# Raw-logit routing with GpSimd refining the norm's scale, and the scan's joined products first

## The reference

```python
x = x + 0.5 * ffn(layernorm(x))
x = x + attn(layernorm(x))
x = x + 0.5 * ffn(layernorm(x))
```

## Time and profile before

| | us |
|---|---|
| median of 3 runs (lowest, highest) | 485.46 (484.73, 485.86) |
| the profiled execution's own time | 485.11 |
| its span, first to last instruction | 483.3 |
| PE busy in the span | 430.8 |
| DVE, ACT, POOL busy | 282.0, 244.2, 236.9 |
| mean granted TensorE clock | 0.951 of full |

### The profile page before, as it was taken

The page is one execution under the profiler, slowest core; times in us unless marked ns, Lnnn a source line. Parts: engine busy times, 40 slices in busy tenths (PEclk is TensorE's granted clock), DMA queues, the critical chain, the costliest instruction groups (busy, mean ns, idle before and its releaser), DMA issues.

```text
span 483.3 us, 9854 instructions
## 1 busy us (share of the span) xinstructions
PE 430.8 (89%) x2877; PEld 354.9 (73%) x2877; DVE 282.0 (58%) x1045; ACT 244.2 (51%) x617; POOL 236.9 (49%) x341
## 2 busy tenths in 40 slices
PE   7999699999908989999999999989989599999940
PEld 5544499999903679999999999974644399999930
DVE  3865355555529657677677777754975245555514
ACT  3693255555510445655655556545786145555520
POOL 4167777544410344465555555642047777454530
PEclk9799999999966999999999999999899999999985
DMA  8971325100065200000000000000001417110028
GB/s 228 263 274 52 111 85 173 34 28 28 18 169 169 64 1 1 2 2 2 1 3 0 1 2 2 2 1 1 2 23 50 117 50 205 35 33 28 20 61 218
DMA packets 34514, 30.90 MB, mean 64 GB/s; under 512 B 3838, under 2 KB 30085, under 8 KB 34464
## 3 DMA queue, kind: packets, MB, share of 16 engines
q1 hardware_dynamic: 24608, 19.17, 14.7%
q0 software_dynamic: 4544, 8.47, 5.4%
q10 hardware_dynamic: 5312, 2.62, 2.1%
HBM read 15.55 MB, written 15.61 MB: 64 GB/s over the span
## 4 chain that ended last, share of the span: by engine, by line
PE 79%; DMA 6%; DVE 4%; POOL 4%; issue 3%; ACT 1%; ACTq 0%; SPq 0%; DVEq 0%; POOLq 0%
PE bank L1275 17%; PE bank L710 15%; PE bank L697 14%; PE bank L658 4%; PE bank L568 4%; DMA stage<-y_dram 3%; POOL slots_dram L1402 3%; PE bank L668 2%; PE bank L1069 2%; PE bank L685 2%; PE bank L1144 2%; PE bank L587 2%; DMA stage<-slots_dram 2%; PE bank L1107 1%; PE bank L1129 1%
## 5 line engine op out<-in xcount | busy, mean ns | idle before, releaser
L1656 DVE TENSOR_TENSOR sq<-bank,relu 128x512 f32<-128x512 f32 x86 | 59.4, 691 | 89.2 <-ACT relu L810 88.9
L1407 POOL DMA_INDIRECT y_dram<-y_out,stage x78 | 76.7, 983 | 59.7 <-ACT y_out L836 52.5
L1402 POOL DMA_INDIRECT slots_dram<-rows,slots x64 | 63.4, 991 | 55.5 <-ACT rows L761 27.2
L710 PE MATMUL bank<-proj_w,sq 128*128 x624 | 86.5, 282 | 2.8 <-DVE sq L1656 2.8
L697 PE MATMUL bank<-tileT,tile_w 128*128 128x128 f32 x624 | 83.1, 277 | 0.0
L710 PEld LDWEIGHTS bank<-proj_w,sq 128*128 128x128 f32 x624 | 75.7, 191 | 6.5 <-issue 3.8
L810 ACT ACTIVATE relu<-bank 128x512 f32<-128x512 f32 x94 | 56.0, 595 | 46.4 <-PE bank L697 37.6
L697 PEld LDWEIGHTS bank<-tileT,tile_w 128*128 128x128 f32 x624 | 76.9, 194 | 0.0
L836 ACT ACTIVATE y_out<-bank,stage 128x128 f32<-128x128 f32 x78 | 28.6, 367 | 33.5 <-PE bank L710 33.5
L1270 POOL TENSOR_TENSOR sq<-sq,last_rows 128x128 f32<-128x128 f32 x32 | 14.6, 456 | 53.0 <-DVE sq L1246 53.0
L568 PE MATMUL bank<-ones 128*128 128x512 f32 x34 | 22.2, 801 | 15.5 <-DVE res L1707 12.6
(11 more groups left out here) (268 smaller groups left out, 1020.5 us busy)
## 6 DMA issues: line engine op xcount, KB each, us to landing
slots_dram<-pad SPq DMA_DIRECT2D x2, 2535.0 KB, 13.8
stage<-slots_dram SPq DMA_DIRECT2D x18, 260.0 KB, 5.1
fc_w<-experts SPq DMA_DIRECT2D x1, 2048.0 KB, 20.5
proj_w<-experts SPq DMA_DIRECT2D x1, 2048.0 KB, 24.1
stage<-y_dram SPq DMA_DIRECT2D x8, 256.0 KB, 5.5
stage<-y_dram ACTq DMA_DIRECT2D x8, 256.0 KB, 6.2
y_dram<-y_out,stage POOLq DMA_INDIRECT x78, 2.3
res<-x SPq DMA_DIRECT2D x4, 256.0 KB, 3.9
```

Of the source, the lines that this page charges most:

```text
L710: last = nc.tensor.matmul(bank[4 + i % 2][:, 0:P], sq[:, i % 2, f_cols], proj_w[:, k, f_cols], start=j == 0, stop=j == FJ - 1)
L1402: nc.gpsimd.indirect_dma_start(to, bass.IndirectOffsetOnAxis(slots[:, n:n + 1], 0), rows[:, k, b, :], None, bounds_check=limit, oob_is_err ...
L1407: nc.gpsimd.indirect_dma_start(y_dram.ap(), bass.IndirectOffsetOnAxis(tiles[:, t, P:P + 1].bitcast(U32), 0), y_out[:, t % YBUFS, :], None, ...
L1656: nc.vector.tensor_tensor(wide_of(i)[2], wide_of(i)[0][:], wide_of(i)[1], ALU.mult)\
```

## The change

Routing: DVE no longer makes the scale. It makes the first guess (`norm_guess`), and GpSimd does the three Newton rounds and `shift` (`pool_scale`, 14 linked operations on 128x16). The routing works on the unscaled logits, in two halves in two PSUM banks, and takes maxima and indices before it waits for the scale; only the gap of the two best is multiplied by it. ACT does the ratio first and its normalised blocks after. The first FFN's counts go ahead of the shared part with one filler call less, the second's from part 4 to part 2.

```diff
-COUNT_AT = (1, 4)
+COUNT_AT = 2
+        def norm_guess(dve, at):
+            dve.wait_ge(dve_step, at[0])
+            dve_link(dve, nc.vector.tensor_scalar(rs_x[:, 0:NBLK], mv[:, :, 1], EPS, None, ALU.add), at)
+            nc.vector.tensor_scalar(rs_h[:], rs_x[:, 0:NBLK], 0.5, None, ALU.mult).then_inc(guess_made, 1)
+            dve_link(dve, nc.vector.tensor_scalar(rs_t[:, 0:NBLK].bitcast(I32), rs_x[:, 0:NBLK].bitcast(I32), 1, None,
+                                                  ALU.logical_shift_right), at)
+            nc.vector.tensor_scalar(rs_y[:, 0:NBLK].bitcast(I32), rs_t[:, 0:NBLK].bitcast(I32), -1.0, float(0x5F3759DF),
+                                    ALU.mult, ALU.add).then_inc(guess_made, 1)
+        def pool_scale(pool, at, f):
+            y, z = rs_y[:, 0:NBLK], rs_z[:]
+            pool.wait_ge(guess_made, 2 * f + 2)
+            for _ in range(3):
+                pool_link(pool, nc.gpsimd.tensor_tensor(z, y, y, ALU.mult), at)
+                pool_link(pool, nc.gpsimd.tensor_tensor(z, z, rs_h[:], ALU.mult), at)
+                pool_link(pool, nc.gpsimd.tensor_tensor(z, one_half[:], z, ALU.subtract), at)
+                pool_link(pool, nc.gpsimd.tensor_tensor(y, y, z, ALU.mult), at)
+            pool_link(pool, nc.gpsimd.tensor_tensor(z, mv[:, :, 0], y, ALU.mult), at)
+            nc.gpsimd.tensor_tensor(shift[:], nothing[:], z, ALU.subtract).then_inc(rstd_done, 1)
...
         def route(dve, at, f):
...
+            for h in range(2):
+                b = slice(h * NBLK // 2, (h + 1) * NBLK // 2)
+                dve.wait_ge(logits_done, 2 * f + h + 1)
+                dve_link(dve, nc.vector.tensor_copy(logits[:, b, :].rearrange("p b e -> p (b e)"),
+                                                    bank[6 - h][:, b.start * E:b.stop * E]), at)
+                for n in range(b.start, b.stop):
+                    last = nc.vector.max(top[:, n, :], logits[:, n, :])
+                dve_link(dve, last, at)
+                for n in range(b.start, b.stop):
+                    last = nc.vector.max_index(topi[:, n, :], top[:, n, :], logits[:, n, :])
             dve_link(dve, last, at)
+            dve_link(dve, nc.vector.tensor_tensor(stat1[:], top[:, :, 1], top[:, :, 0], ALU.subtract), at)
+            dve.wait_ge(rstd_done, f + 1)
+            nc.vector.tensor_tensor(below[:], stat1[:], rs_y[:, 0:NBLK], ALU.mult).then_inc(below_done, 1)
...
-            pe_keep_busy(2)
+            pe_keep_busy(1)
+            pe_counts(pe, 0)
             pe_tiles(pe, 0)
```

```diff
         def pe_offset(pe, step, turn):
-                nc.tensor.matmul(x.t_bank[:, 0:2 * P], x.offset, ident_zero, start=True, stop=False)
+                ins = mm(x.t_bank, x.offset, ident_r, start=False, stop=step.old is None)
...
         def pe_yrows(pe, step, turn):
-                nc.tensor.matmul(x.t_bank[:, 0:2 * P], x.a, w2_ident[:, 0:2 * P], start=False, stop=True)\
+                nc.tensor.matmul(x.t_bank[:, 0:2 * P], x.a, w2_ident[:], start=True, stop=False)
...
         def pe_da_old(pe, step):
-                nc.tensor.matmul(x.d_bank[:, 0:2 * P], x.ee[:, old.to, :], zero_rows, start=True, stop=False)
+                mm(x.d_bank[:, P:2 * P], x.ee[:, old.to, :], x.rows[:, 0:P], start=False).then_inc(x.da_done, 1)
...
                 if early:
-                    pe_offset(pe, early[0], turn)
                     pe_aa(pe, early[0], turn)
                 pe_inner(pe, late[0])
                 if early:
                     pe_y(pe, early[0], turn)
                     pe_yrows(pe, early[0], turn)
+                    pe_offset(pe, early[0], turn)
                 pe_da_old(pe, late[0])
...
                 pe_th_transposed(pe, late[1])
                 if early:
+                    pe_aa(pe, early[1], turn)
+                pe_da_old(pe, late[1])
+                if early:
+                    pe_yrows(pe, early[1], turn)
                     pe_offset(pe, early[1], turn)
-                    pe_aa(pe, early[1], turn)
                     pe_old_guess(pe, early[1])
-                pe_da_old(pe, late[1])
-                if early:
-                    pe_yrows(pe, early[1], turn)
                     pe_y(pe, early[1], turn)
                 pe_da(pe, late[1])
...
                 if early:
-                    pe_da_old(pe, early[1])
                     pe_inner(pe, early[1])
                 pe_w1_sums(pe, late[1], upd1_done)
                 pe_w2_sums(pe, late[1])
                 pe_b1_sums(pe, late[1], upd1_done)
                 if early:
                     pe_da(pe, early[1])
+                    pe_da_old(pe, early[1])
                 pe_w2t_sums(pe, late[1], upd2_done)
```

More of the change, by code:

```diff
@@ L194, in mk_macaron @@
         rs_x = sb("rs_x", [P, NBLK * TOPK])
+        rs_h, rs_z, one_half, nothing = (sb(n, [P, NBLK]) for n in ("rs_h", "rs_z", "one_half", "nothing"))
         rs_y = sb("rs_y", [P, NBLK * TOPK])
@@ L719, in pe_tiles @@
                     packed.append(expert_word(pe, f, word_at(i)))
-                if i == COUNT_AT[f]:
+                if f and i == COUNT_AT:
                     pe_counts(pe, f)
@@ L787, in act_ffn @@
                 act_ratio(act, f)
-                for b in range(2, ROWS_FIRST[f]):
+                act.wait_ge(rstd_done, 1)
+                for b in range(ROWS_FIRST[0]):
                     act_normalised(b)
@@ L849, in act_tiles @@
                     squared(i)
-                if i == 1 and f == 1:
+                if i == 0 and f == 1:
                     act_ratio(act, f)
+                    act.wait_ge(rstd_done, 2)
+                    for b in range(ROWS_FIRST[1]):
+                        act_normalised(b)
                 b = ROWS_FIRST[f] + i
@@ L1030, in pe_offset @@
             if x is ahead:
-                if step.n:
-                    pe.wait_ge(x.erows_done, step.n)
-                wait_param(pe, step, turn, "w2")
-                nc.tensor.matmul(x.t_bank[:, 0:2 * P], x.offset, ident_zero, start=True, stop=False)
+                ins = mm(x.t_bank, x.offset, ident_r, start=False, stop=step.old is None)
+                if step.old is None:
+                    ins.then_inc(x.yrows_done, 1)
             else:
@@ L1045, in pe_old_guess @@
             pe.wait_ge(old.chain.aa_done, old.m + 1)
-            mm(x.t_bank if x is ahead else x.d_bank, old.chain.aa[:, old.to, :], old.chain.ed[:, old.to, 0, :],
-               start=False, stop=False)
+            ins = mm(x.t_bank if x is ahead else x.d_bank, old.chain.aa[:, old.to, :], old.chain.ed[:, old.to, 0, :],
+                     start=False, stop=x is ahead)
+            if x is ahead:
+                ins.then_inc(x.yrows_done, 1)
         def pe_yrows(pe, step, turn):
@@ L1128, in pe_da @@
             if x is ahead:
-                nc.tensor.matmul(x.d_bank[:, 0:2 * P], x.e, e_w2t[:], start=step.old is None, stop=True)\
-                  .then_inc(x.da_done, 1)
+                if step.n:
+                    pe.wait_ge(x.d_done, step.n)
+                ins = nc.tensor.matmul(x.d_bank[:, 0:2 * P], x.e, e_w2t[:], start=True, stop=step.old is None)
+                if step.old is None:
+                    ins.then_inc(x.da_done, 1)
             else:
@@ L1344, in _ @@
                 nc.gpsimd.memset(digit[:, :, n], float(8 ** n))
+            nc.gpsimd.memset(one_half[:], 1.5)
+            nc.gpsimd.memset(nothing[:], 0.0)
             nc.gpsimd.memset(ones[:], 1.0).then_inc(consts_made, 1)
@@ L1464, in _ @@
                 part(NBLK)
+            pool_scale(pool, at, 1)
             pool_tiles(1)
@@ L1884, in _ @@
                 pe_key_part(pe, *key_part(5 * step.n))
+                pe_yrows(pe, step, -1)
                 pe_offset(pe, step, -1)
@@ L1887, in _ @@
                     pe_old_guess(pe, step)
-                pe_yrows(pe, step, -1)
                 pe_aa(pe, step, -1)
@@ L1962, in _ @@
                 if early:
-                    pe_offset(pe, early[1], turn)
                     pe_aa(pe, early[1], turn)
-                    pe_old_guess(pe, early[1])
                 pe_da_old(pe, late[1])
@@ L1968, in _ @@
                     pe_yrows(pe, early[1], turn)
+                    pe_offset(pe, early[1], turn)
+                    pe_old_guess(pe, early[1])
                     pe_y(pe, early[1], turn)
```

77 lines of the change are left out of this document (32 added, 45 removed).

## The result

The changed kernel takes 489.05 us (median of 21 runs, 487.44 to 491.29) against 486.18 for the kernel before (21 runs beside them, 484.73 to 489.21). The ratio is 1.006, 95% interval 1.0045 to 1.0074: 2.9 us slower, where I forecast 1.9 us faster. The profiled execution of the changed kernel took 491.02 us (span 488.9, against 483.3 before), 2 us above its median, so not everything in its trace is typical of the kernel.

The account below looks back on a forecast made before the run. TensorE had 79% of the chain; in the FFNs, when the slots are known sets the routed tiles' start. 485.11 - 1.7 (first FFN) - 2.55 (second) + 2.7 (scan) = 483.56, stated as 483.6 us; range 482 to 485, without far ends 479.5 to 487.5.

Parts of the forecast that it names:

- The scan, +2.7: Scan: products moved out of PE's holes cost 0.18 us in each of 15 turns, +2.7 us.
- the same 0.2: Scan turn: late chain's `da` 0.18 later and early `da_old` adding about 0.1 are one delay, not two.
- My upper bound, 0.31 a turn: Scan's upper bound: 0.31 a turn plus 0.2 for each of three opening steps, +5.3 us.
- The first FFN, -1.7: First FFN: slots known 1.95 to 2.05 us earlier, little room on PE; -1.7, bounds -2.4 and 0.
- the hole of about a microsecond: First FFN: PE's idle before the counts, which may hold back the high clock by some 512-column passes.
- The second FFN, -2.55: Second FFN: counts read 2.15 us earlier plus -0.4 for the clock; -2.55, bounds -3.4 and 0.
- The 2.15: Second FFN: counts read at about 349.35 instead of 351.50, 2.15 us earlier.
- The -0.4 for the clock at the tiles: Second FFN, first gathered tiles: a shorter PE hole may keep the clock; about half of 0.81 us, -0.4.
- the two widths equal as slots: Scan: 128 fewer columns save only 0.01 us per product, since moving columns hide behind the next weight load.
- nothing in the first half of the turn: Scan, first half of a turn: `offset` moves from one hole to another, costing nothing.
- rival 3: Both FFNs: GpSimd becomes the bound and DVE waits, both routings losing 3.2 us; time 490.2, chance 0.12.
- Rival 4: Scan loses +5.3 (486.2), or the cold clock takes the FFN gains (first FFN at 0: 485.3); chance 0.16.

Follow-up runs that it names:

- either mended: Two kernels, each the changed kernel with one edit: d_bank as before (ratio to before 1.0036), or `yrows`, `offset`, `old_guess` issued right behind `aa` (1.0005).
- with both: Changed kernel with d_bank as before and also `yrows`, `offset`, `old_guess` issued right behind `aa`: ratio to the kernel before 0.9961.
- routing alone: Changed kernel without the scan's hunks, so its routing with the scan as before: ratio to the kernel before 0.9964.
- scan alone: Kernel before with only the scan's hunks of the change: ratio to the kernel before 1.0115.
- two fillers, add behind `upto`: Changed routing, scan as before, GpSimd's add waiting for `upto`, two filler calls before the first counts instead of one: ratios to before 0.9921 and 0.9933.

## Why the prediction was wrong

- **The scan, +2.7: the step that failed.** "Both paths say 0.2, the same 0.2, not twice." They are twice: 0.19 from the three products that left the hole ahead of the final chain's `da_old`, and 0.11 to 0.12 from the early `da_old` put between `da` and its readers. The runs with either mended, and with both, show the two apart and adding up; 0.34 a turn instead of 0.18, +5.1 instead of +2.7. My upper bound, 0.31 a turn, lies next to the measured 0.34, but I took it for a far end. In the profile of the changed kernel the final chain's loads from its `da` on, and the early `da`, are 0.21 to 0.22 later against the `aa` load than before; what stands behind the early `da_old`, the final chain's last sums and the early chain's sums, is 0.27 to 0.33 later. The second delay is laid on a stream that the first had already made late, and the next turn starts from its end.
- **The first FFN, -1.7: nothing came.** In the six kernels with the routing as changed, `reached` is between 20.89 and 22.09 in the profile and the first tiles between 54.27 and 55.21; in the two with the old routing 20.64 and 21.85, 53.26 and 54.44. Counted from the first scale step, which itself moves by 0.8 us between executions, `reached` comes after 9.1 to 9.7 us (old: 9.1 and 9.75) and the first tile after 42.5 to 43.2 (old: 41.7 and 42.3). Three things stand against the gain. The first is shown by the run with the add moved; what the other two cost is read from the traces, and no run separates them. First, DVE lost 1.0 us to GpSimd's add, which I had queued behind the scale and taken for free: `below` or `chosen`, whichever falls beside it, ends only after the add has (add 16.74 + 1.26 = 18.00, `below` 18.03; add 18.63 + 1.27 = 19.90, `chosen` 20.18). In the kernel before, the same add ran at 16.73 beside FIND_INDEX8 and cost nothing. The changed order put a two-input TENSOR_TENSOR of DVE there. Second, "the hole of about a microsecond" was 1.5 to 5.2 us in these six, and at the low clock it was 1.5 to 1.7 us from the first counting product to `reached` (19.52 to 21.05 in the routing alone), against 0.97 in the changed kernel's own profile, where the clock was up. Third, PE became the later one at the first tile (in the routing alone it waits again, 0.57 us, for the next group).
- The Trainium skill has the rule for the first of these, on the page "SBUF — State Buffer", section "Who interferes with whom": a DVE instruction with two SBUF inputs and a GpSimd instruction that reads SBUF exclude each other, and the one that issues second waits for the first to end. This case's trace agrees: 1.14 and 1.45 us beside the add, 0.17 and 0.43 without it. The rows of FIND_INDEX8 name two tiles as well (`top` and `logits`), and it was not held; a MATCH_VALUE_LOAD stands ahead of each, and the trace does not show which of the two reads which tile.
- **The second FFN, -2.55: right in its place, too large.** The 2.15 is there in the profiled pair (7.62 against 9.78 to `reached`). Over the eleven profiles with the new routing the first tile comes 40.0 to 41.8 us after the first scale step, 40.65 in the mean, against 42.33 and 41.84 with the old: 1.2 to 1.7 us. In three of the eleven PE's logits and first fc's ran at the low clock and `reached` was at 8.8. The -0.4 for the clock at the tiles did not come: the first 16 L728 took 2.80 to 3.25 us in ten of these profiles and 3.62 in the changed kernel's own, against 2.99 before and 3.62 in the scan alone.
- **Right:** GpSimd's 0.22 us an operation and its 4.1 us in all, DVE not waiting for it, the length of DVE's new chain once the add is out of its way (12.20 to 18.77 with the add behind `upto`: 6.57 us, forecast 6.58), the two widths equal as slots, nothing in the first half of the turn, and the wait in part 8 of the shared expert gone.
- **Slips in the working:** by its own terms rival 3 has -2.55 + 3.2 = +0.65 in the second FFN, not +0.9; and rivals 3 and 4, from which the 0.2 for slower is made, add up to 0.28.
- **Sum:** +5.1 + 0 - 1.7 = +3.4; measured +2.9 (2.2 to 3.6). Rival 4 described the scan's loss and the lost first FFN as alternatives; both came.
- **Not settled:** why PE's clock in the first 20 us, at 180 to 200 and at the start of the second FFN differs between executions of one kernel. Around the first turn the changed kernel took 19.03 us from the third opening `aa` to the second turn's (173.69 to 192.72), against 17.54 before and 17.63 in the scan alone, with a granted clock of 0.91 at 180 to 200 (1.00 in the other two); the routing alone, 19.06, has the same dip. Nor is it explained why in all eleven profiles with the new routing the first half of the second turn takes 4.09 us or 4.10 instead of 3.84.

## What to carry to other kernels

When a product is moved out of a hole in an in-order stream, add up the delays of every chain that later meets it; two delays are the same one only if both chains wait for the same instruction at the end. Before work is put on GpSimd, or DVE's order around a GpSimd operation is changed, lay the two timelines side by side and look at which DVE operations with two inputs would fall beside it. Filler of a fixed amount covers a wait only if it happens to run during it; look at more than one execution before you count on it.

## What the hardware showed that was not expected

- GpSimd and DVE exclude each other by operation: a 128x512 add on GpSimd (1.26 us) held a 128x16 DVE product from 0.17 to 1.14 us, and a 128x256 one from 0.43 to 1.45. FIND_INDEX8 ran beside it in the kernel before at its usual pace (one in 0.135 us), and MAX8 and FIND_INDEX8 ran beside the 14 small GpSimd operations without loss (a half of the routing in 2.03 us, worked out beforehand as 2.02).
- A linked chain on GpSimd steps at 0.30 us for 128x16 with two inputs (0.22 of work); DVE's linked steps take 0.21.
- Two executions of one kernel (two fillers, add behind `upto`) reach the first gathered tile at 53.08 and 54.60, and the one with the higher granted clock from 10 to 20 us (0.92 against 0.66) is the later: its filler ends early, PE idles 2.86 us, and its first eight shared fc products take 6.09 us instead of 3.67, with a granted clock from 20 to 30 us of 0.74 against 1.00.
